# A token's variance made in 64 equal columns by each of its products in place of one column

## The reference, cut to what matters

```python
# block 0: batch norm, 1x1 projections, 4 heads of 32 channels, 1024 x 1024 scores, residual
x = _L0_conv_ref(x, ...)
t = _to_tokens(x)                          # (8, 1024, 128)
# block 1: 64 heads of 2 channels, q and k rms-normed, causal softmax, residual
t = t + _L1_attn_ref(_ln_t(t), ...)
# block 2: 8 experts of three 128 x 128 layers, weighted by a softmax gate, residual
t = t + _L1_ffn_ref(_ln_t(t), ...)

def _ln_t(v, eps=1e-05):                   # over the 128 channels of a token
    m = jnp.mean(v, axis=-1, keepdims=True)
    s = jnp.var(v, axis=-1, keepdims=True)
    return (v - m) / jnp.sqrt(s + eps)
```

## Time and profile before

| what | value |
|---|---|
| time, median of 3 runs | 3389.75 us (3385.29 to 3397.03) |
| profiled execution, its own time | 3398.41 us |
| its span | 3396.7 us |
| mean granted clock of TensorE | 0.974 |
| busy share PE, PEld, DVE, ACT, POOL | 91%, 32%, 61%, 80%, 8% |

### The profile page before, as it was taken

The page is one execution under the profiler, slowest core; times in us unless marked ns, Lnnn a source line. Parts: engine busy times, 40 slices in busy tenths (PEclk is TensorE's granted clock), DMA queues, the critical chain, the costliest instruction groups (busy, mean ns, idle before and its releaser), DMA issues.

```text
span 3396.7 us, 70341 instructions
## 1 busy us (share of the span) xinstructions
PE 3078.5 (91%) x27633; PEld 1087.3 (32%) x27633; DVE 2062.5 (61%) x2974; ACT 2711.0 (80%) x2580; POOL 263.9 (8%) x350
## 2 busy tenths in 40 slices
PE   6899999999798898998999899899998988999999
PEld 3444444444322222222222222222222222233444
DVE  4788878888656456556556556656656643443333
ACT  5444444445499999999999999999999999973555
POOL 6000000000110011011010110101101000000000
PEclk9899999999899999999999999999999999998999
DMA  6121211120100110210210210210210211001000
GB/s 224 53 53 44 53 47 34 44 52 20 53 16 18 59 26 18 61 27 17 59 29 18 59 27 20 59 27 17 60 29 18 59 27 37 19 15 63 13 12 12
DMA packets 132542, 135.73 MB, mean 40 GB/s; under 512 B 27414, under 2 KB 111476, under 8 KB 132220
## 3 DMA queue, kind: packets, MB, share of 16 engines
q1 hardware_dynamic: 131216, 130.44, 13.9%
q10 hardware_dynamic: 1004, 0.83, 0.1%
HBM read 70.31 MB, written 51.41 MB: 36 GB/s over the span
## 4 chain that ended last, share of the span: by engine, by line
ACT 39%; PE 35%; issue 19%; DVE 5%; DMA 1%; SPq 1%; ACTq 0%; POOL 0%; DVEq 0%
ACT arena L961 38%; PE ps L1318 5%; PE ps L1371 3%; PE ps L1040 3%; PE ps L1365 3%; PE ps L1087 3%; PE ps L1406 3%; PE ps L1114 3%; PE ps L1089 3%; PE ps L1098 2%; PE ps L1069 2%; PE ps L1270 2%; DVE arena L1480 1%; DVE arena L1487 1%; DVE arena L1492 1%
## 5 line engine op out<-in xcount | busy, mean ns | idle before, releaser
L961 ACT ACTIVATE arena<-ps 128x1536 f32<-128x1536 f32 x1536 | 2068.3, 1636 | 21.6 <-PE ps L1270 21.2
L1318 PE MATMUL ps<-arena 128*32 128x512 f32 (+3 forms) x12288 | 1257.8, 504 | 1.9 <-DVE arena L1755 1.7
L1755 DVE TENSOR_TENSOR arena<-arena,causal 128x512 f32<-128x512 f32 x1024 | 664.5, 688 | 314.1 <-ACT arena L961 304.6
L1270 PE MATMUL ps<-arena 15*128 15x512 bf16 (+3 forms) x6144 | 606.9, 331 | 160.7 <-ACT arena L961 151.1
L890 ACT ACTIVATE arena<-ps 128x512 f32<-128x512 f32 x512 | 299.8, 596 | 278.8 <-PE ps L1089 268.2
L1270 PEld LDWEIGHTS ps<-arena 15*128 15x128 bf16 x6144 | 163.0, 92 | 1100.6 <-ACT arena L961 958.7
L1318 PEld LDWEIGHTS ps<-arena 128*32 128x32 f32 x12288 | 284.7, 109 | 385.1 <-issue 331.4
L1480 DVE TENSOR_REDUCE arena<-ps 128x32 bf16<-128x1024 f32 x256 | 311.2, 1216 | 119.9 <-PE ps L1069 119.9
L1487 DVE TENSOR_TENSOR arena<-arena,ps 128x512 f32<-128x512 f32 x512 | 329.2, 680 | 33.5 <-PE ps L1098 32.6
L1740 DVE COPY arena<-ps 128x512 f32<-128x512 f32 x256 | 176.5, 690 | 219.9 <-PE ps L1318 218.9
L1087 PE MATMUL ps<-arena 96*128 96x256 bf16 x1024 | 260.7, 279 | 0.3 <-ACT arena L863 0.2
(11 more groups left out here) (200 smaller groups left out, 1970.9 us busy)
## 6 DMA issues: line engine op xcount, KB each, us to landing
arena<-qstack SPq DMA_DIRECT2D x512, 30.0 KB
parts<-arena SPq DMA_DIRECT2D x8, 1536.0 KB, 6.3
arena<-parts SPq DMA_DIRECT2D x48, 256.0 KB, 5.4
arena<-parts SPq DMA_DIRECT2D x96, 128.0 KB, 2.8
arena<-kstack SPq DMA_DIRECT2D x512, 24.0 KB
qstack<-arena SPq DMA_DIRECT2D x24, 384.0 KB, 3.3
attn<-arena SPq DMA_DIRECT2D x512, 12.0 KB
arena<-arena SPq DMA_DIRECT2D x384, 16.0 KB, 1.8
```

Source lines behind the costliest of these rows:

```text
L961: act.activation(PR1[:, at:at + CW], bank(BPC * (f % 2), BPC), ACT.Exp).then_inc(d_exp, 1)
L1270: mm = pe.matmul(bank(at + k)[:, s * P:(s + n) * P], Ks[par][HR * h:HR * h + QROWS, j * P:(j + 1) * P], Qs[par][HR * h:HR * h + QROWS, t * ...
L1318: mm = pe.matmul(o[HR * h:HR * (h + 1), :], V1[n % 2][:, j, v:v + HR], pr[:, h * HALF + s * P:h * HALF + (s + k) * P], start=not opened[hi ...
L1755: dve.tensor_tensor(v, v, m3, ALU.min).then_inc(d_mask, 1)
```

## The change

The moving operand becomes the first VC = 64 columns of `mean_w`. All its elements are equal, so the 64 columns that come out of a product are equal too, and a block of tokens takes 64 columns of the bank in place of one. The eight blocks fill the bank's 512 columns (VC = HALF // NT). The readers take the first of each block's 64 columns. Nothing else is touched.

```diff
+VC = HALF // NT
+
+
+def variances(o, at, n):
+    return o.rearrange("p (t c) -> p t c", c=VC)[:, at:at + n, 0:1].rearrange("p t c -> p (t c)")
...
-                    act.activation(dev0, bank(2)[:, 0:NT], ACT.Sqrt, bias=eps_c[:, 0:1]).then_inc(c0_act, 1)
+                    act.activation(dev0, variances(bank(2), 0, NT), ACT.Sqrt, bias=eps_c[:, 0:1]).then_inc(c0_act, 1)
...
                 for t in blocks:
-                    mm = pe.matmul(o[:, t:t + 1], squares[:, t * P:(t + 1) * P], mean_w[:, 0:1], start=True, stop=True)
+                    mm = pe.matmul(o[:, t * VC:(t + 1) * VC], squares[:, t * P:(t + 1) * P], mean_w[:, 0:VC],
+                                   start=True, stop=True)
                 mm.then_inc(t_sem, 1)
...
-                    dve.tensor_scalar(dv[:, at:at + NT // 2], o[:, at:at + NT // 2], LN_EPS, None, ALU.add)\
+                    dve.tensor_scalar(dv[:, at:at + NT // 2], variances(o, at, NT // 2), LN_EPS, None, ALU.add)\
...
-                    dve.tensor_scalar(ev[:, at:at + NT // 2], o[:, at:at + NT // 2], LN_EPS, None, ALU.add)\
+                    dve.tensor_scalar(ev[:, at:at + NT // 2], variances(o, at, NT // 2), LN_EPS, None, ALU.add)\
```

## The result

The changed kernel takes 3374.14 us (median of 6 runs, 3369.59 to 3376.11) where the kernel before took 3388.26 (3385.29 to 3397.03, 6 runs): ratio 0.996, 95% interval 0.9945 to 0.9974, 14.1 us less. It is faster by more than the 0.3% that can be told apart. The forecast was 3379, with a range of 3371 to 3391. The runs also lie closer together than before.

The account below looks back on a forecast made before the run. The prediction took ACT's exponentials to bound the long stage, with PE's clock falls making ACT wait. Clock -10.6 us plus 0.1 us of PE time in the tail gave -10.5, so 3389.75 became 3379 us, range 3371 to 3391.

Parts of the forecast that it names:

- ACT sets the pace of the long stage: Long stage: ACT busy 2067.97 of 2088 us with exponentials; PE changes can only save from some 20 us of waits.
- The one-column passes bring the falls behind variance: Long stage: clock falls behind ten of 28 variance pieces, costing 10.6 us of ACT's time; 64 columns should remove all ten.
- The control of the prediction: Long stage: 14 pieces v0 and v1, same form with 128 columns, showed no clock fall, against ten of 28 variance pieces.
- The term for the clock: Long stage: all ten clock falls behind variance pieces go, -10.6 us, bounds 0 to 17.5 us gained.
- upper bound of 17.5 us: Long stage: most the clock could give, if all 14 va1 at about 1.15 us and two va0 at 0.68 were hit.
- Falls elsewhere: Long stage: seven falls following no variance piece may become none or twice as many, -4.8 to +4.8 us; taken as 0.
- PE's time: Variance pieces: 0.05 us more each, 1.4 us in the long stage, hidden by PE's lead; 0.1 us paid in the tail.
- rival D: Variance pieces: columns and weight loads don't overlap, 0.43 us more each, 12.0 us in all, 3402 us; chance 0.05.
- Readers and the short stage: DVE's readers stay at 162 ns despite the step of 64; short stage taken as 0, bound -1.2 us.
- A: Variance pieces: 64 columns don't do and the clock falls as before, 3390 us, in part 3385; chance 0.17.
- B: Long stage: the ten falls go but eight new ones come elsewhere, -5.2 us, 3385 us; chance 0.10.
- C: More spared: usual falls exceed the profile's and the short stage gains, -15 to -17 us, 3374 us; chance 0.06.

Follow-up runs that it names:

- values_narrow: Changed kernel with v0 and v1 of the long stage making one column of values per token block in place of 128: 3384.11 us, ratio 0.9991 to the kernel before.
- va1_only: Changed kernel with 64 columns only in pieces va1 of long stage and tail, one column in va0 and short stage: 3371.85 us, ratio 0.9959 to the kernel before.
- late_va1: Changed kernel's bank places, but one column in every product and va1 moved to slot 1 of its group in the long stage: 3372.42 us, ratio 0.9947.
- second comparison: The changed kernel, unaltered, timed once more against the kernel before: 3372.06 us, ratio 0.9942 (0.9929 to 0.9956).
- short_only: Changed kernel with 64 columns in the short stage alone, one column in long stage and tail: 3387.04 us, ratio 0.9997 to the kernel before.
- filler: Changed kernel with one column in every variance product, plus an unread 256-column float32 product ahead of each va1: 3383.47 us, ratio 0.9995 to the kernel before.
- cols_128: Changed kernel with 128 columns per variance product in the long stage and tail, 64 in the short stage: 3372.18 us, ratio 0.9941 to the kernel before.

## Why the prediction was right, and where it was off

- *ACT sets the pace of the long stage, and its waits for PE are all there is to gain.* Right: the stage's gain is 13.2 us of waits and the restarts behind them.
- *The one-column passes bring the falls behind variance, and 64 columns spare them.* Right: ten of 28 before, none in six profiles with 64 columns or more throughout, back behind v0 when v0 is narrowed. The control of the prediction, ten of 28 against none of 14, pointed the right way, but was weaker than the text made it. v1 doesn't wait for the copy, so only the seven v0 are like va1. And the counts aren't so many separate trials: E's va1 come 259.4 us apart from 1416 to 2454 and so do their five falls, one meeting repeated, while six of C's seven va1, with one column and the same wait, were spared as v0 was. What settled it was values_narrow. The prediction also named only the passes, and the runs show two conditions: va1 alone gives the gain (va1_only), and moving it to slot 1, away from the wait, gives it with no columns (late_va1). The profile had it: eight of the ten falls stood behind va1, which waits for the copy, and the two behind va0 stood behind a wait for ACT.
- *The term for the clock, -10.6 us,* was the mis-sized one. It counted ACT's waits, 1.17 us for a fall, where a fall costs 1.38, so ten are 12.6 us. The timed difference is 14.1 us, and 16 in the second comparison. The prediction's upper bound of 17.5 us had room for that through more falls per execution. The runs show dearer falls, and falls at other pieces in other executions: short_only's eight behind va1 cost 10.8 us of waits, two of them being long ones, as much as the ten here. That the profiled execution stood for the others although it was one of the slowest was in part luck. The 1.5 to 3.5 us beyond 12.6 may be falls elsewhere, the next point; no run shows it.
- *Falls elsewhere, taken as 0, -4.8 to 4.8.* In the profiles 3.5 us fewer. Profiles of the other kernels have two to eight such falls, so part of this is chance, and how much isn't settled.
- *PE's time, 0.05 us for a piece, hidden.* Right: 1.04 us against 0.99, with ACT at 8.00 of 8. The cover was thinner than the text made it: filler shows a lead of 0.28 us at va1. 0.05 fits; the 0.43 of rival D would not have.
- *Readers and the short stage, nothing.* Right: 162 ns, and 0.9997 for short_only.
- *Rivals.* A, that 64 don't do, is out; with 32 columns it would have been half true. B and D are out. C, more than the profile's falls, is where the time came to lie in part, 15 to 17 us being its number. Of its two reasons, the gain in the short stage is out (short_only), and a higher usual count of falls isn't shown.

On the rule that a weight load runs beside products in flight only for other rows of the array (the Trainium skill, "TensorE: Matmul & The Clock Gate", Part 3): cols_128 disagrees again, for full-array float32 passes with 128 columns: eight take 1.09 us to the next scores, 0.10 more than with one column.

Left open: how often each piece is hit over many executions, since each kernel has one or two profiles; whether it is the wait for the copy or the place in the group that makes va1 and v0 the pieces that are hit; why some falls last longer; and the eight other falls of late_va1.

## What to carry to other kernels

Where one engine is busy all the time and TensorE runs just ahead of it, look at the granted clock in windows of a few us behind each narrow product that follows a wait: a fall there turns the lead into waits. Widen the moving operand where weight loads set the pace anyway, or move the narrow work to another place; a product added beside it costs what is beyond TensorE's lead (0.15 of 0.43 us here, and 0.1 for the restart), each time. Price a fall by the instructions done in a stretch, not by the idle time, since the engine also loses its overlap at each restart.

## What the runs showed that was not expected

Identical sequences met a fall in one image or execution and not in another. Runs of the kernel before spread over 18 us (3380.43 to 3398.79 in one comparison) and those of the changed kernel over 6. The Trainium skill says in "TensorE: Matmul & The Clock Gate", Part 1, that the activity monitor runs freely; the rows agree. An exponential of 128x1536 costs 1.45 us alone and 1.34 in a row.
